# Mixture-of-experts stage of a two-layer network: input turned in two halves, routing earlier, the next sequence's rows normalised on ScalarE

## The reference, cut to what matters

```
xn = layernorm(x)                                    # per row of 256
s  = L1_attn(xn)       # RWKV-like: token shift, LoRA mixes, 32 state scans, per-head group norm, silu gate, @ oW
f  = L1_ffn(xn)        # below
x  = x + s * silu(f)

def L1_ffn(x):                                       # 16 heads of attention, then experts
    x = x + attention(rmsnorm(x))
    h = rmsnorm(x)
    logits = h @ Wgate + bias                        # 8 experts, the 2 highest, softmax over those 2
    out = sum over e of comb[:, e] * ((silu(h @ Wg[e]) * (h @ Wu[e])) @ Wd[e])     + the shared expert
    return x + out
```

## Time and profile before

| | |
|---|---|
| median of three runs | 2258.83 us |
| the profiled execution | 2257.5 us, span 2255.7 us |
| mean granted TensorE clock | 0.957 of full |
| TensorE busy (matmul) | 2057.1 us, 91% |
| VectorE busy | 1758.3 us, 78% |
| ScalarE busy | 976.9 us, 43% |
| GpSimd busy | 836.6 us, 37% |

### The profile page before, as it was taken

One profiled execution on the slowest core, in us unless ns is written; L12 is line 12 of the kernel. 1 busy time (PEld: TensorE's weight loads), 2 busy tenths in 40 slices (PEclk: granted clock), 3 DMA queues, 4 the chain that ended last, 5 costly groups with the idle time before them and its releaser, 6 DMA issues.

```text
span 2255.7 us, 37286 instructions
## 1 busy us (share of the span) xinstructions
PE 2057.1 (91%) x11722; PEld 1245.7 (55%) x11723; DVE 1758.3 (78%) x2906; ACT 976.9 (43%) x2556; POOL 836.6 (37%) x666
## 2 busy tenths in 40 slices
PE   7998599998998999999899989998998999899887
PEld 4554499997455445544554555455455545554553
DVE  5997466664598879778886988798789869887985
ACT  2544244442375247234623651373247236623731
POOL 1335200001443354435334542643354335336421
PEclk9999799998899999999999999999999999999998
DMA  6554422113213013211221220122022211211310
GB/s 173 148 151 143 148 54 56 55 53 100 76 55 83 10 51 78 70 38 43 67 52 42 61 84 11 44 80 76 22 54 67 56 43 53 65 40 42 77 51 10
DMA packets 145727, 151.18 MB, mean 67 GB/s; under 512 B 47664, under 2 KB 105648, under 8 KB 145584
## 3 DMA queue, kind: packets, MB, share of 16 engines
q1 hardware_dynamic: 138288, 136.73, 22.3%
q0 software_dynamic: 3072, 8.41, 1.2%
q10 hardware_dynamic: 4224, 4.19, 0.7%
HBM read 121.71 MB, written 27.43 MB: 66 GB/s over the span
## 4 chain that ended last, share of the span: by engine, by line
PE 33%; issue 20%; DVE 13%; POOL 7%; ACT 3%; DMA 0%; POOLq 0%; DVEq 0%; ACTq 0%
PE bank L1379 11%; PE bank L1238 5%; PE bank L1255 4%; PE bank L1292 3%; POOL arena L2063 3%; PE bank L1392 3%; DVE arena L1778 2%; ACT arena L1584 2%; DVE arena L1791 2%; PE bank L1265 2%; PE bank L1171 2%; DVE arena L1798 2%; PE bank L1241 1%; DVE arena L2005 1%; POOL arena L2055 1%
## 5 line engine op out<-in xcount | busy, mean ns | idle before, releaser
L2055 POOL TENSOR_TENSOR arena<-arena 128x512 f32<-128x512 f32 x256 | 354.8, 1387 | 586.4 <-DVE arena L1798 560.2
L1379 PE MATMUL bank<-arena 128*128 128x512 f32 (+2 forms) x1312 | 442.7, 492 | 6.8 <-DVE arena L1923 6.8
L1171 PE MATMUL bank<-arena 128*128 128x512 f32 (+2 forms) x768 | 361.1, 617 | 24.3 <-DVE arena L1722 17.9
L1379 PEld LDWEIGHTS bank<-arena 128*128 128x128 f32 x1312 | 254.3, 208 | 179.9 <-issue 148.9
L1798 DVE TENSOR_TENSOR_SCAN arena<-arena 128x512 f32<-128x512 f32 x256 | 350.0, 1367 | 1.8
L1584 ACT ACTIVATE arena<-bank,arena 128x128 f32<-128x128 f32 (+3 forms) x512 | 266.1, 529 | 191.8 <-DVE arena L1778 191.8
L1791 DVE TENSOR_TENSOR arena<-arena 128x512 f32<-128x512 f32 x256 | 239.5, 936 | 39.8 <-DMA arena<-values 27.2
L1171 PEld LDWEIGHTS bank<-arena 128*128 128x128 f32 (+2 forms) x768 | 141.0, 191 | 217.9 <-issue 175.1
L1238 PE MATMUL bank<-arena 64*128 64x128 f32 (+3 forms) x1024 | 208.8, 484 | 55.3 <-ACT arena L1584 52.0
L1778 DVE TENSOR_REDUCE arena<-bank 128x2 f32<-128x256 f32 (+3 forms) x256 | 207.2, 810 | 23.4 <-PE bank L1241 22.9
L1593 ACT ACTIVATE arena<-bank 128x128 f32<-128x128 f32 (+3 forms) x512 | 196.1, 438 | 39.5 <-PE bank L1255 39.0
(11 more groups left out here) (200 smaller groups left out, 2906.6 us busy)
## 6 DMA issues: line engine op xcount, KB each, us to landing
arena<-values SPq DMA_DIRECT2D x256, 256.0 KB, 3.5
arena<-in_L_attn_h SPq DMA_DIRECT2D x16, 512.0 KB, 4.8
arena<-in_W1T SPq DMA_DIRECT2D x8, 1024.0 KB, 5.1
arena<-in_W2T SPq DMA_DIRECT2D x8, 1024.0 KB, 9.0
sorted_rows<-arena SPq DMA_DIRECT2D x42, 128.5 KB, 10.5
arena<-sorted_rows SPq DMA_DIRECT2D x40, 128.5 KB, 2.1
arena<-in_b2row SPq DMA_DIRECT2D x40, 128.0 KB, 3.0
gate_rows<-arena SPq DMA_DIRECT2D x39, 128.0 KB, 1.7
```

The source lines that it names most:

```text
L1171: last = nc.tensor.matmul(dst[rows, :], w, x, start=(n == 0), stop=(n == len(pairs) - 1))
L1379: last = nc.tensor.matmul(dst[o], w, x, start=first, stop=last_one)
L2055: nc.gpsimd.tensor_tensor(prods[(n + 2) % PRODS], state[n % STATES][:, 0:T], proj["r"][:, m, :], ALU.mult).then_inc(prod_done, 1)
```

## The change

The experts' input goes through in halves: transposes, copies, gate and the two products of expert 0, each first for rows 0 to 255. The last reduction of the attention stage (group 4) and the matmul `var0` move behind the first half's transposes. On VectorE `hidden(0)` goes into the middle of the routing, before its tail. State unit 22 goes behind both halves, 23 behind the routing, 24 and 25 behind expert 0; GpSimd's gather comes behind product 24 as before. The next rows are normed on ScalarE (`norm_head`, from `s_in`, scale and bias per row) instead of VectorE; the square sum is replaced by var * rstd * rstd from the statistics. `head_lerp` moves one expert forward. The group norm of y's first half moves from `between(6)` to `between(8)` into the next sequence's blends (only the last sequence keeps it in `between`). ScalarE's silu of the expert sum moves behind the first three tanh of the next sequence. `la_d` is made before `mean_last` and the blends' products.

```diff
+EXPERT_UNITS = {0: (24, 25), 1: (26,), 2: (27,), 3: (28,), 4: (29,), 5: (30, 31)}
+REDUCED = ((2, 5), (5, 6), (ME, 7))          # was (2, 5), (4, 6), (ME, 7)
 # TensorE, before_attention
 lora_a("vk", 0, 2)
 lora_a("rg", 2, 2)
+lora_a("d", 4, 1)
 mean_last(ended)
 lora_pair(b, "v", "k", th[0])
-lora_a("d", 4, 1)
 # TensorE, attention: no reduce_state(4) ahead of wo(0, [3]), no var0 ahead of wo(2, [3])
 # TensorE, experts
+turn_rows(0)
+reduce_state(b, 4)
+result(b, "var0", ...)
+gate_tiles(0)
+for name, w in first: up_half(name, w, 0)
+turn_rows(1)
+gate_tiles(1).then_inc(made2, 1)
+for name, w in first: up_half(name, w, 1).then_inc(made2, 1)
 # ScalarE
+def norm_head(b):
+    if b:
+        act.wait_ge(v_read2, post.read(b - 1, "d0b"))
+    act.wait_ge(shift_done, b + 1)
+    for i in range(NT):
+        last = nc.scalar.activation(xn[:, i, :], s_in[:, i, :], ACT.Identity, scale=rstd[:, i:i + 1], bias=shift[:, i:i + 1])
 if e == ME - 2 and not final:
-    square_head(b + 1)
+    norm_head(b + 1)
+def bring_rows(half):     # on VectorE one for bank xc{half}0, on ScalarE one for xc{half}1, 256 columns each
 # VectorE, end of attention
 add_rows(1)
+bring_rows(0)
+norm_rows(1)
+bring_rows(1)
 scan(b, EARLY)
-norm_rows(1)
-(one copy of 512 columns)
 # VectorE, experts: the routing first, then
 nc.vector.tensor_tensor(routs[4], best[0], best[1], ALU.subtract).then_inc(comb_in, 1)
+hidden(0)
 (tail of the routing)
+outer(b, EARLY + 1)
+for n in range(EARLY + 1, EXPERT_UNITS[0][0]): unit(b, n)
 def between(e):
+    if not final:      # ahead of the units
+        if e == 1: head_gate(b + 1)
+        elif e == 2: head_sum(b + 1)
+        elif e == 3: head_stats(b + 1)
+    for n in EXPERT_UNITS.get(e, ()): unit(b, n)
+    if not final:
+        if e == 4: head_shift(b + 1)          # four operations on 128x4
+        elif e == 6: head_lerp(b + 1)
+    elif e == 6: ln_inv(b, 0)
+    elif e == 7: ln_scale(b, 0), ln_gate(b, 0)
 # VectorE, before_attention
 for name in ("v0", "k0", "v1", "k1"): blend(name)
+ln_inv(ended, 0)
 for name in ("d0", "d1", "r0", "g0", "r1", "g1"): blend(name)
+ln_scale(ended, 0)
+ln_gate(ended, 0)
 # VectorE, the last (shared) expert: two sums of 512 columns instead of four of 256
 # GpSimd, experts
-product(b, EARLY + 1)
-product(b, EARLY + 2)
+for n in range(EARLY + 1, EXPERT_UNITS[0][-1]): product(b, n)
 gather(b + 1)
+(rstd behind product 28, rms behind product 29; was ahead of product 30 and behind the last)
```

More of the change, by code:

```diff
@@ L1436, in experts @@
                         for i in (2 * half, 2 * half + 1):
[L1437 to L1442, removed]
+                            last = nc.tensor.transpose(bank[post.bank(f"xc{half}{k}")][:, (i % 2) * P:(i % 2 + 1) * P],
+                                                       xb[:, i, k * P:(k + 1) * P], ident)
@@ new lines, in turn_rows, with gate_tiles, up_half @@
+                    last.then_inc(made2, 2)
+                def gate_tiles(half):
+                    dst = bank[post.bank("gate")]
+                    for i in (2 * half, 2 * half + 1):
+                        for k in range(KD):
+                            last = nc.tensor.matmul(dst[:, i * ME:(i + 1) * ME], xbT[:, k, i * P:(i + 1) * P], gate_w[:, k, :],
+                                                    start=(k == 0), stop=(k == KD - 1))
+                    return last
+                def up_half(name, w, half):
+                    cols = slice(2 * P * half, 2 * P * (half + 1))
+                    for k in range(KD):
+                        last = nc.tensor.matmul(bank[post.bank(name)][:, cols], w[:, k, :], xbT[:, k, cols],
+                                                start=(k == 0), stop=(k == KD - 1))
+                    return last
@@ new lines, in experts @@
+                turn_rows(0)
+                reduce_state(b, 4)
+                pe.wait_ge(sq_done, 2 * b + 1)
+                result(b, "var0", [(full, mean_m, sq[0], True, True)], bank[post.bank("var0")])
+                pe.wait_ge(v_read2, post.read(b, "xc00"))
+                pe.wait_ge(a_read2, post.read(b, "xc01"))
+                pe.wait_ge(moe_in, 16 * 3 * (ME + 1))
+                begin(b, "gate", post, post_read)
+                gate_tiles(0)
+                first = (("g0", eg_w[0]), ("u0", eu_w[0]))
@@ L1560, in before_attention @@
                 if ended is not None:
+                    silu_rows(ended)
                     root_last(ended)
@@ L1983, in between @@
                         ln_scale(b, 0)
-                    elif e == 8:
                         ln_gate(b, 0)
+                    if e == ME:
                         read_out(b, 1)
-                    for at, part in ((1, head_gate), (2, head_sum), (3, head_stats), (4, head_norm), (6, head_ms), (7, head_lerp)):
-                        if e == at and not final:
-                            part(b + 1)
-                hidden(0)
+                outer(b, EARLY + 1)
+                for n in range(EARLY + 1, EXPERT_UNITS[0][0]):
+                    unit(b, n)
                 for e in range(ME + 1):
@@ L2101, in experts @@
             def experts(b, final):
-                product(b, EARLY + 1)
-                product(b, EARLY + 2)
+                for n in range(EARLY + 1, EXPERT_UNITS[0][-1]):
+                    product(b, n)
                 if not final:
```

152 lines of the change are left out of this document (88 added, 64 removed).

## The result

The changed kernel takes 2191.72 us (median of 4 runs, 2188.28 to 2194.1), beside 2257.11 for the kernel before (median of 4 runs); the ratio is 0.9717, 95% interval 0.9692 to 0.9742. A later set of 5 runs gave 0.9729 (0.971 to 0.9748). The forecast was 2182, so 65 us were won where 76 were expected; the measured time lies inside the forecast's range of 2163 to 2220 and inside its narrow one of 2172 to 2198. The profiled execution took 2192.86 us, span 2191.0, mean granted clock 0.975 instead of 0.957.

What follows compares the result with a forecast made beforehand. TensorE was taken to bound phase c. Seven middles of 10.5 us (73.5) plus 6.15 for the last sequence, less 1.75 and 1.7, gave 76.2 us saved: 2182, range 2163 to 2220, narrow range 2172 to 2198 (chance 0.57).

Steps and rivals of the forecast that it cites:

- Entry: Experts' input to the end of up(1): one wait of 0.6 us left, up(1) ends at 1346.0, 7.9 us earlier.
- 0.16 of doubt: Rival at the experts' entry: the clock falls there all the same; price 37 us, 2219; chance 0.16.
- hidden(0): VectorE, in the routing: done at 1345.1, ahead of up(1)'s end at 1346.0, so down(0) isn't held up.
- The gather's wait: VectorE before head_gate: gather lands at 1360.5, a stall of about 3.2 us; TensorE then waits 1.4 for down(3).
- my own sign: In the experts: the forecast is wrong if TensorE waits for hidden over 2 us a sequence.
- the stage of the experts: TensorE through the experts: 2.55 us of idle time goes, 1.95 of waits come, 0.6 gained a sequence.
- a rival (2188): GpSimd's gather: by the shared port rule its four issues lengthen about 1 us in all, 2188; no separate chance given.
- norm_head: ScalarE in the experts: four operations of 1.71 us, 1378.4 to 1380.1, ahead of the transposes at 1380.5; table load taken as 0.
- Into the next sequence: Next sequence's blends: 1.7 us of clock and 0.68 of wait saved, 0.4 of new waits, net 2.0 gained.
- the forecast's first rival: Experts: gather lands by 1357.2 or VectorE's slack absorbs it, TensorE bound throughout; 15 us less, 2167; chance 0.13.
- The slower rival: Down(3) and after: new waits lower the clock, each fall up to 5.1 us; three a sequence give 2289; chance 0.04.
- The forecast's price: TensorE at low clock, busy with float32 matmuls of 512 columns: it loses about half of each such stretch.

Runs made afterwards that it cites:

- units_first: The changed kernel with units 23 and 24 ahead of the routing on VectorE, 25 and 26 behind expert 0, gather behind product 24: 0.9814, 2212.1 us.
- ln_back: The changed kernel with the first half of the group norm back in the experts instead of among the next blends: 0.9875, 2225.8 us.
- gather_first: The changed kernel with GpSimd's gather ahead of products 23 and 24 instead of behind them: 0.9585, 2161.5 us.
- gather_first_ln_back: The changed kernel with the gather ahead of products 23 and 24, and the group norm's first half back in the experts: 0.9719 of the kernel before.
- gather_first_gap_filled: gather_first with TensorE's reduction of group 4 moved from behind the first half's transposes to behind the second half's: 0.9553, 2152.6 us.
- after_again: The changed kernel unchanged, run again as the mark for the other runs: 0.9729 of the kernel before, 2193.4 us.

## Why the forecast was nearly right, step by step

The fourth sequence of the kernel after is compared by adding 24.54 us, the difference of a landmark that the change doesn't touch (`spread_inverse`, at 1326.41 in the kernel before and at 1301.87 in the changed one). Forecast values are in brackets.

- **Entry.** First transposes at 1333.0 (1333.2), wait for the copies 0.66 (0.6), up(1) ended at 1345.5 (1346.0), clock 1.00 (1.00). The gate takes 0.95 for a half, where I had taken 1.2 of a range of 0.9 to 1.8. Right. That the clock would stay up was given 0.16 of doubt, rightly: with two waits of 0.58 and 0.89 in place of the one it falls in 6 of 8. One of my arguments for it was wrong, though. I had read that the waits of up to 1.5 us in attention go with a granted clock of 1.00; in the sixth sequence of the kernel before one doesn't:

```profile
1881.62 1.15 PE L1238 MATMUL bank<-arena 64*128 64x256 f32 x4 [1.46 <-ACT arena L1584]
```

```profile
1878.00:1888.00 10.00, 8.39 (x52) 5.22 (x50) 7.92 (x9) 7.50 (x27) 4.73 (x3) 0.83 0.29 85
```

- **hidden(0)** done at 1344.5 (1345.1). Right, and shown to be necessary by `units_first`.
- **The gather's wait** was seen in the diff and forecast, with 3.2 us. It is 4.9. This is the term that was mis-sized. The product ended 0.4 earlier than forecast (1328.4 + 24.5 = 1352.9 against 1353.3), but the copy of the indices took 1.11 instead of the old 0.18 and the next operation 0.58 instead of 0.20, beside VectorE's scan and `outer`. The last issue came 5.8 us behind the copy's start and not 4.5, the landing 2.9 after it: 1361.7 (1360.5). VectorE was there 0.5 earlier than forecast. TensorE waited 2.96 before down(3) and not 1.4. I had written that I would be wrong if TensorE waited for `hidden` over 2 us a sequence: it waits 21.5 in seven, 3.1 each. So by my own sign the stage of the experts was wrong, though the total was near.
 The Trainium skill, page "SBUF — State Buffer", section "Terms", says of the port pair that VectorE and GpSimd share that the loser blocks for the whole instruction. The trace agrees for the small operations: the copy ends at 1329.49 and VectorE's scan at 1329.51, the next operation at 1330.15 and `outer` at 1330.09. By that rule I had put the gather about 1 us later in a rival (2188), by longer issues. The size was near by luck: none of the 32 issues took over 1.07 us, as before the change, and the 1.3 us came in the two operations ahead of them.
- **VectorE sets the pace from there on.** I had TensorE as the bound of the experts, with short waits. VectorE has no pause from `head_gate` to `hidden(8)`, and falls further behind the forecast by its own parts: `hidden(3)` done at 1365.3 (1363.9), `hidden(5)` at 1376.2 (1374.9), `hidden(6)` at 1381.8 (1379.7), `hidden(8)` at 1392.6 (1390.1). Of these 2.5 us, 1.2 are the gather's landing. Some 0.8 are the four small operations of `head_shift`, of which the first took 1.26 us and not 0.2; it ends at 1356.22 and GpSimd's product beside it at 1356.20. The rest is longer scans beside products and rounding.
- **`norm_head`** takes 2.08 us for four operations instead of 1.71, behind the late first operation of `head_shift`:

```profile
1356.31 2.08 ACT L1535 ACTIVATE arena<-arena 128x256 f32<-128x256 f32 x4 [4.68 <-DVE arena L1751]
```

 TensorE waits 0.62 for it, where I had none, but only in the three sequences whose clock doesn't fall at down(3); the four others reach the same point later, wait for nothing there, and take the same 199.8 us. So this wait costs nothing as long as VectorE is the bound. No function table is loaded for `norm_head`; the Trainium skill, page "ScalarE: Activation LUTs", section "Table sets: the hidden batching unit", says that identity is in every set, and the trace agrees.
- **Start of the next sequence** at 1394.5, forecast 1392.0: 2.5 us late, as `hidden(8)` is.
- **Into the next sequence**: from the first product to the end of the w products it was 26.6 us and is 24.2, 2.4 less where 2.0 were forecast, with no wait for the blends behind `ln_inv(0)`. Right. What VectorE does there is covered, and `ln_back` prices what it would cost elsewhere.
- **The account.** A sequence was to gain 7.9 at the entry, 0.6 in the experts and 2.0 into the next sequence, 10.5 in all. It gained 8.2 (down(0) begins at 1353.7 before and at 1345.5 after), lost 2.2, and gained 2.4: 8.4. So the experts' stage is the step that failed, by 2.8 us a sequence: 20 us in seven, of which the entry and the blends gave 5 back. From the first sequence's transposes to the last one's it is 55.4 us less, where the forecast had 7 x 10.5 - 3.5 = 70. Ahead of them 2.8 instead of 1.9 was won, behind them 6.4 instead of 4.25; the stretch ahead differs by up to 4 us among the runs whose code is the same there, so that this part is within the noise. Together that makes the difference between 76.2 and 64.6.
- **Without the stall** the forecast's first rival had 2167, 15 us less; `gather_first` took 2161.5, 32 less. I had priced a stall of 3.2 us on VectorE at 2.2 a sequence, as TensorE would have been the bound without it; it costs its whole length.
- **Low clock inside the experts.** The slower rival asked for it and it came, once a sequence: 3.4 us behind the wait for `hidden(3)`, in four of seven sequences (window 738 to 748 above: 0.83). But those sequences take 199.8 us like the others. The forecast's price, half of each such stretch, is wrong here: it is nothing as long as VectorE is the bound. What `gather_first` gained, 32 us, is VectorE's wait alone (33.5).

Not tested by themselves are the earlier `head_lerp`, the earlier `la_d` and the later silu. That the waits of 2.55 and 0.68 us which they were to remove are gone is seen in the trace; which edit did it, and what each is worth, isn't shown.

## What to carry to other kernels

When work is reordered on one engine, follow every product of it through the other queues: a gather that stands behind product 24 had landed 10 us ahead of its user and came 4.9 us behind it, because unit 24 moved; its place on GpSimd was worth 32 us, half as much as the whole change. Ask which engine sets the pace behind a wait before pricing it: a wait on that engine costs its whole length, and low clock or a short wait on the other costs nothing there, as the sequences of 199.8 us with and without them show. At the entry, where TensorE sets the pace, a wait cost its length and the half clock behind it, and the gap was best filled with reductions and small matmuls that are due anyway. When two engines end a stage together, work added to VectorE lengthened it in full (`gather_first_ln_back`), and an edit pays that brings both forward (`gather_first_gap_filled`). Work moved to where the bound engine idles counts in full: 33 us for one inverse and two products.

## What the runs showed of the hardware

The clock's fall depends on more than the longest idle time: waits of 0.58 and 0.89 us with four transposes between them and the short gate matmuls behind were followed by 3.4 us at half clock in 6 of 8 sequences, while the wait of 0.66 in the changed kernel never was (1.00 in all eight). In attention, which I had taken to be safe, a wait of 1.46 us was followed by such a stretch in the sixth sequence of the kernel before, in the seventh of the changed one, and in none of these seven in `after_again`, which is the same kernel. Extra matmuls of constants in an idle gap made the kernel before 12 us faster. Tiny GpSimd or VectorE operations on 128x4 are not tiny beside the other engine's large ones: 0.18 became 1.11 us and 0.2 became 1.26, each ending within 0.02 us of the large operation beside it. The issues of the indirect DMAs, 0.95 us each, were not lengthened, not even in `gather_first`, where a scan of VectorE (1308.15 to 1309.43) runs beside the last one (1308.09).
